# A three-phase transformer block on one core: the experts' first rows are added to x by accumulating transfers from GpSimd

## The reference, cut to what matters

```python
def reference(x, ...):                          # x: 32 x 256 x 128, float32 (8192 tokens)
    x = x + 0.5 * ffn(layernorm(x), ...)        # phase f1: 8 experts, 2 of them per token
    x = x + attn(layernorm(x), ...)             # phase at
    x = x + 0.5 * ffn(layernorm(x), ...)        # phase f2: as f1
    return x

def ffn(x, rw1, rb1, rw2, rb2, we1, be1, we2, be2):
    logits = silu(x @ rw1 + rb1) @ rw2 + rb2    # the two best of 8 experts per token
    w = softmax over the two best
    return x + sum over e of w[e] * (silu(x @ we1[e] + be1[e]) @ we2[e] + be2[e])

def attn(x, g1, b1, Wq, Wk, Wv, Wo, g2, b2, Wf1, Wf2):   # 32 sequences of 256 tokens
    x = x + linear_attention(layernorm(x, g1, b1))       # 16 heads of 64, causal
    return x + gelu(layernorm(x, g2, b2) @ Wf1) @ Wf2
```

## Time and profile before

| | |
|---|---|
| time, median of 3 runs | 2164.51 us (2164.07 to 2168.26) |
| the profiled execution, its own time | 2165.33 us |
| its span (first to last instruction) | 2163.3 us |
| granted TensorE clock, mean of the span | 0.923 |
| busy: TensorE, VectorE, ScalarE, GpSimd | 1727.8, 1517.6, 1041.2, 914.0 us |
| phase f1, at, f2 (from the timeline) | until about 509, to about 1610, to 2163 us |

### The profile page before, as it was taken

One profiled execution on the slowest core, in us unless ns is written; L12 is line 12 of the kernel. 1 busy time (PEld: TensorE's weight loads), 2 busy tenths in 40 slices (PEclk: granted clock), 3 DMA queues, 4 the chain that ended last, 5 costly groups with the idle time before them and its releaser, 6 DMA issues. The chain is left out here.

```text
span 2163.3 us, 36059 instructions
## 1 busy us (share of the span) xinstructions
PE 1727.8 (80%) x12483; PEld 1397.8 (65%) x12483; DVE 1517.6 (70%) x4134; ACT 1041.2 (48%) x1833; POOL 914.0 (42%) x1020
## 2 busy tenths in 40 slices
PE   3442999993999999999999999999954444999970
PEld 2331777772788888888888888888843333777750
DVE  6663777774787888788788887887636653777753
ACT  1210766663556555565555555565521112666650
POOL 5775355555322222222222222222106773555560
PEclk9999999996999999999999999999965556999995
DMA  5535576651000000000000000000001115666637
GB/s 163 184 127 178 183 251 232 231 184 51 6 11 11 6 11 11 6 11 11 7 11 11 6 11 11 2 1 2 2 0 40 48 49 187 229 217 232 224 122 235
DMA packets 89309, 190.28 MB, mean 88 GB/s; under 512 B 15869, under 2 KB 54442, under 8 KB 78122
## 3 DMA queue, kind: packets, MB, share of 16 engines
q1 hardware_dynamic: 60202, 141.68, 19.6%
q0 software_dynamic: 18176, 37.79, 5.1%
q10 hardware_dynamic: 10752, 8.52, 1.2%
HBM read 131.08 MB, written 56.85 MB: 87 GB/s over the span
## 5 line engine op out<-in xcount | busy, mean ns | idle before, releaser
L503 POOL DMA_INDIRECT expert_rows<-f_rows_out,f_dest x312 | 311.4, 998 | 291.3 <-DVE f_rows_out L722 218.4
L1178 POOL TENSOR_TENSOR at_sc<-at_sc 128x512 f32<-128x512 f32 x128 | 168.6, 1317 | 496.1 <-DVE at_sc L1283 496.1
L435 ACT ACTIVATE f_hid<-f_up_ps,f_w 128x512 f32<-128x512 f32 x312 | 214.7, 688 | 170.6 <-PE f_up_ps L344 160.5
L1275 DVE SCALAR_TENSOR_TENSOR at_qk<-at_exps,at_relus 128x512 f32<-128x512 f32 x256 | 192.4, 752 | 145.5 <-ACT at_relus L1114 145.2
L497 POOL DMA_INDIRECT sent_rows<-f_xn,f_slot x256 | 250.4, 978 | 92.3 <-issue 74.7
L1283 DVE TENSOR_TENSOR at_sc<-at_s_ps,at_mask 128x384 f32<-128x384 f32 x512 | 251.6, 549 | 1.2 <-PE at_s_ps L985 1.2
L699 DVE TENSOR_TENSOR f_hid_lo<-f_hid,f_hid_hi 128x512 fp32r<-128x512 f32 x312 | 208.2, 689 | 14.3
L982 PE MATMUL at_s_ps<-at_qk 64*128 64x256 f32 x1024 | 171.2, 411 | 7.0 <-issue 5.6
L1158 ACT ACTIVATE raw<-at_num_ps 128x512 f32<-128x512 f32 x128 | 76.3, 596 | 206.0 <-PE at_num_ps L1002 206.0
L1113 ACT ACTIVATE at_exps<-at_proj_ps 128x512 f32<-128x512 f32 x253 | 152.1, 601 | 34.7 <-PE at_proj_ps L965 27.6
L997 PE MATMUL at_num_ps<-at_sc,at_vals 128*64 128x256 f32 x1024 | 161.1, 393 | 0.3 <-DVE at_den L1360 0.3
(11 more groups left out here) (238 smaller groups left out, 4633.7 us busy)
## 6 DMA issues: line engine op xcount, KB each, us to landing
f_w<-split_weights SPq DMA_DIRECT2D x78, 1028.0 KB, 5.0
f_got<-sent_rows SPq DMA_DIRECT2D x78, 264.0 KB, 4.7
split_weights<-f_split SPq DMA_DIRECT2D x8, 1024.0 KB, 4.5
at_taken<-expert_rows SPq DMA_DIRECT2D x64, 128.0 KB, 2.1
f_w<-expert_rows SPq DMA_DIRECT2D x32, 256.0 KB, 4.0
expert_rows<-f_rows_out,f_dest POOLq DMA_INDIRECT x312, 3.3
sent_rows<-f_pads ACTq DMA_DIRECT2D x16, 264.0 KB
x<-in_L_attn_x SPq DMA_DIRECT2D x16, 256.0 KB, 4.1
```

Of the source, the lines that this page charges most:

```text
L435: A(hid[:, c, :], up_ps[n % 4][:, :], ACT.Silu, bias=w[:, i % RING_W, 4 * HID + c:4 * HID + c + 1].bitcast(FP32)).then_inc(s_silu, 1)
L503: g.indirect_dma_start(out=k.back[:, :], out_offset=bass.IndirectOffsetOnAxis(dest[:, i % RING_DEST, q:q + 1], 0), in_=rows_out[:, i % RIN ...
L1178: g.tensor_tensor(sc[:, n % RING_SC, :, 3, :], sc[:, n % RING_SC, :, 1, :], sc[:, n % RING_SC, :, 2, :], ALU.add).then_inc(s_sum, 1)
L1275: stt(full, exps[:, p % 2, :], 1.0, relus[:, p % 2, :], ALU.min, ALU.add).then_inc(s_phi, 1)
```

## The change

The loads by SP, the ring `taken` and GpSimd's additions go. In their place GpSimd issues, for each block, two transfers from `expert_rows` straight onto the block of `k.x` in SBUF, with `accum_op=ALU.add`: the transfer itself reads x, adds and writes. The second of a block waits on GpSimd until the first has landed (both touch the same bytes). One semaphore of four, `s_added[i % 4]`, counts 16 for each transfer, so 32 per block. In the loop the first part of block s + 3 is issued at unit 1 of step s and the second at unit 3. VectorE waits for 32 more on the block's semaphore where it waited for `s_added` before.

```diff
--- before.py
+++ after.py
@@ -764,7 +764,6 @@
     return sems
 
 
-RING_TAKEN = 4
 RING_SC = 6
 
 
@@ -823,15 +822,13 @@
         h2_hi, h2_lo = sb("h2_hi", [P, BT], FP32R), sb("h2_lo", [P, BT], FP32R)
         gel = sb("gel", [P, HC, BT])
         warm = sb("warm", [P, 2])
-        taken = sb("taken", [P, RING_TAKEN, 2, BT])
 
         s_ps = [ps(f"s{i}") for i in range(4)]
         proj_ps, num_ps, slot_ps = [ps(f"proj{i}") for i in range(2)], ps("num"), ps("slot")
 
         s_split_hi, s_split_lo, s_const, s_head_sel = (
             sem("split_hi"), sem("split_lo"), sem("const"), sem("head_sel"))
-        s_taken = [sem(f"taken{i}") for i in range(RING_TAKEN)]
-        s_first, s_added = sem("first"), sem("added")
+        s_added = [sem(f"added{i}") for i in range(4)]
         s_st = {n: sem(f"st{n}") for n in "ABC"}
         s_mv = {n: sem(f"mv{n}") for n in "ABC"}
         s_ve = {n: sem(f"ve{n}") for n in "ABC"}
@@ -891,16 +888,6 @@
             return ap.rearrange("p a b -> p (a b)")
 
         block = ctx.enter_context(nc.Block())
-
-        @block.sync
-        def _(sp):
-            for i in range(NB):
-                if i >= RING_TAKEN:
-                    sp.wait_ge(s_added, i - RING_TAKEN + 1)
-                for j in range(2):
-                    first = j * TOKENS + i * BT
-                    sp.dma_start(taken[:, i % RING_TAKEN, j, :],
-                                 k.back[first:first + BT, :].rearrange("(p q) d -> p (q d)", q=BQ)).then_inc(s_taken[i % RING_TAKEN], 16)
 
         @block.tensor
         def _(pe):
@@ -1177,15 +1164,17 @@
                 pool.wait_ge(s_masked, 2 * n + 2)
                 g.tensor_tensor(sc[:, n % RING_SC, :, 3, :], sc[:, n % RING_SC, :, 1, :], sc[:, n % RING_SC, :, 2, :], ALU.add).then_inc(s_sum, 1)
 
-            def add_back(i):
-
-                pool.wait_ge(s_taken[i % RING_TAKEN], 32 * (i // RING_TAKEN + 1))
-                g.tensor_tensor(k.x[:, xc(i)], k.x[:, xc(i)], taken[:, i % RING_TAKEN, 0, :], ALU.add).then_inc(s_first, 1)
-                pool.wait_ge(s_first, i + 1)
-                g.tensor_tensor(k.x[:, xc(i)], k.x[:, xc(i)], taken[:, i % RING_TAKEN, 1, :], ALU.add).then_inc(s_added, 1)
-
-            add_back(0)
-            add_back(1)
+            def add_back(i, j):
+
+                if j:
+                    pool.wait_ge(s_added[i % 4], 32 * (i // 4) + 16)
+                first = j * TOKENS + i * BT
+                g.dma_start(k.x[:, xc(i)], k.back[first:first + BT, :].rearrange("(p q) d -> p (q d)", q=BQ),
+                            accum_op=ALU.add).then_inc(s_added[i % 4], 16)
+
+            for j in range(2):
+                for i in range(2):
+                    add_back(i, j)
             inverse_std("A", 1)
             inverse_std("B", 1)
             inverse_std("A", 2)
@@ -1216,8 +1205,9 @@
                                     pattern=[[-1, UNITS], [-32, 2], [0, DH]], channel_multiplier=1).then_inc(s_const, 1)
             g.affine_select(out=low_rows_4[:, :], in_=low_rows_4[:, :], compare_op=ALU.is_ge, fill=0.0, base=31,
                             pattern=[[32, 4]], channel_multiplier=-1).then_inc(s_const, 1)
-            add_back(2)
+            add_back(2, 0)
             sum_blocks(0)
+            add_back(2, 1)
 
             for s in range(NB + 2):
                 for u in range(UNITS):
@@ -1230,8 +1220,8 @@
                         inverse_std("B", s + 3)
                     if u == 2 and has_rest(s):
                         inverse_std("C", s)
-                    if u == 3 and s + 3 < NB:
-                        add_back(s + 3)
+                    if u in (1, 3) and s + 3 < NB:
+                        add_back(s + 3, u // 2)
                 if s == 0:
                     nc.clear_and_free_semaphores(spent)
                     pool.sem_inc(k.cleared, 1)
@@ -1309,13 +1299,13 @@
                 return lambda q: k.x[:, xc(i, q)]
 
 
-            dve.wait_ge(s_added, 1)
+            dve.wait_ge(s_added[0], 32)
             first_mean("A", 0, x_of(0))
             low(0)
             normalise("A", 1, y_of(0), x_of(0), s_y)
             dve.wait_ge(s_y, 1)
             first_mean("B", 0, y_of(0))
-            dve.wait_ge(s_added, 2)
+            dve.wait_ge(s_added[1], 32)
             first_mean("A", 1, x_of(1))
             normalise("B", 1, lambda q: z[:, q, :], y_of(0), s_z)
             low(1)
@@ -1353,7 +1343,7 @@
                     if g + 1 < LAST:
                         mask_scores(2 * (g + 1))
                     if u == 0 and ahead:
-                        dve.wait_ge(s_added, s + 3)
+                        dve.wait_ge(s_added[(s + 2) % 4], 32 * ((s + 2) // 4 + 1))
                         stats("A", lambda q: k.x[:, xc(s + 2, q)])
                     if u == 0 and rest:
                         dve.wait_ge(s_quad, s)
```

## The result

The changed kernel takes 2169.8 us (median of 20 runs), the kernel before 2166.4 us in the same comparison (20 runs): ratio 1.0015, 95% interval 1.0009 to 1.0022, so 3.4 us longer, with 1.9 to 4.8 us in the interval. It is a small loss, 0.15% of the time, and clear of zero.

A forecast was written before the change was run, and what follows sets the result against it. The prediction took TensorE's own instructions to bound the attention phase, one pass in 32.8 us. Only the start counted, so 2164.5 + 0.6 = 2165.1 us; own range 2163.5 to 2171, 8 in 10 from 2162 to 2183.

The forecast's parts named there:

- The sum: Whole kernel: removed additions 0, issues 0, 29 passes 0, start +0.6 us, added to the median of 2164.5 us.
- Passes: 29 steady passes of the step loop: x may land up to 4.5 us after issue at no cost; value 0.
- the removed additions: GpSimd in the step loop: 32 pairs of 1.66 us, 53 us, end before idle time; value 0.
- the issues: GpSimd in the step loop: two DMA issues per pass, about 2 us, hidden in idle time; value 0.
- the landing: Steady passes: second transfer lands 3.2 us after issue, with 4.0 us of room before stats A; value 0.
- Rival (b): Steady passes: removing GpSimd's additions frees VectorE time that reaches TensorE, gaining 0.5 us a pass, 14.5 us; chance 0.06.
- Rival (c): GpSimd's transfer issue is held up by VectorE, landing at 3.6 us, +1.4 us, 2166; part of the forecast's 0.74.
- L: Time from start of a transfer's issue to landing in SBUF, sum made: 3.2 us taken, upper bound 4.6.
- The estimate of 2.6 us: Accumulating transfer by the Trainium skill: 2.0 + 0.6 us, which would turn the start into a 0.6 us gain.
- The start: Start of attention phase: two transfers in series before block 0's stats A; normalise at 517.9 against 517.26, +0.6 us.
- Rival (a): Stats A in every steady pass: landing above 4.5 us makes the kernel slower, +18.7 us at 5.0; chance 0.20.
- The slack: Steady passes: another 0.5 us behind the 4.0 us of room, before TensorE's broadcast at 1028.03 is late.

The follow-up runs named there:

- price: Changed kernel plus extra GpSimd transfers into unused columns; landing 2.6, 3.1 and 4.1 us for 64, 128 and 256 KB accumulated; no ratio given.
- half_start: Changed kernel, but second rows of blocks 0 and 1 loaded by SP and added by GpSimd; ratio 0.9987, stats A at 4.74 us.
- low_after: Changed kernel with VectorE's low(0) moved behind normalise of block 0; no ratio, first reciprocal at 59.96 us, last write of x at 1103.46 us.
- delay3: Changed kernel with three 0.9 us GpSimd memsets ahead of each pass's second transfer; last write of x +44.5 us against after_again.
- base_again: Unchanged copy of the kernel before, run again on later chips; ratio 1.0014 (0.9995 to 1.0033).
- after_again: Unchanged copy of the changed kernel, run again on later chips; ratio 1.0010 (0.9989 to 1.0031).
- order: Kernel before, with GpSimd's additions of block 1 moved behind inverse_std A of block 0 and low(0) behind its normalise; ratio 1.0005 (0.9989 to 1.0021).

## Why the prediction was right, and which of its terms were off

**The number.** The sum gave +0.6 us and the measurement +3.4. It stayed inside the forecast of 0.2% (4.3 us) because the range was wide enough for terms at the start that the sum had too small, not because the sum was close. A further 1.9 us of the distance between 2165.1 and 2169.8 is the reference: the kernel before has a median of 2164.5 in the three runs at hand and 2166.4 in the twenty of the comparison.

**Passes: right.** Value 0 for the removed additions (0.5 us of VectorE given back to its wait for ScalarE), 0 for the issues (0.9 us each, nobody behind them late), 0 for the landing (3.1 us taken in 4.0 us of room). Rival (b), a gain through VectorE, is refuted by the pass of 32.8 us. Rival (c), an issue held up by VectorE, doesn't show: the longest issue, 1.25 us, is the second of the phase, while VectorE is idle, and block 2's second issue, which starts at 542.13 beside VectorE's cast (L1330, 540.97 to 542.73), takes 0.90 us and lands after 3.1.

**L: right within 0.1 us.** 3.2 taken, 3.1 measured. The rows for twice the bytes gave a good value for this size; that twice the bytes is the reason, price doesn't show. The estimate of 2.6 us from the Trainium skill (DMA: Bandwidth & Descriptors, "Anatomy of one DMA", with Collectives: The Full Stack, "The bandwidth ceiling: the fold count and why AG ≠ RS ≠ AR") was 0.5 us short: its 2.3 us for a plain transfer of 128 KB agree with the 2.4 of L1237, but its two fetched sources don't cover the rest.

**The start: right in mechanism, short in size.** +0.6 was the sum, +2.1 us the measured shift of normalise. In the sum's own terms, from ScalarE's first instruction: GpSimd's first issue stands at 0.47 us, where -0.04 was taken (+0.5); the first transfer lands after the 3.2 us that were taken, but the issue that waits for it comes 0.26 us behind it instead of 0.1 (+0.2); from there to stats A 3.14 instead of 3.23 (-0.1); and from stats A to normalise 2.77 instead of 1.88 us (+0.9). The last is the mis-sized term. rs_A was laid under low(0), at its undisturbed duration; beside low(0), which reads two operands from SBUF, ve_A took 1.08 us and not 0.19. A row at hand had shown the same: the addition L1185 takes 1.69 us beside low(0) and 0.73 in a pass. The Trainium skill has this (SBUF — State Buffer, "Who interferes with whom": a VectorE instruction with two SBUF inputs contends with a GpSimd instruction that reads SBUF), and the runs agree: 1.08 beside it, also in half_start, where an addition and not an issue stands ahead of ve_A, and 0.19 without it in low_after. The prediction used the section for GpSimd's issues and not for its small operations. low_after also shows that taking these 0.9 us out doesn't shorten the phase, since low(0) itself then stands in the chain. And the prologue doesn't move as one, as the prediction had it: the shift of 2.1 us at normalise is 1.8 at the first reciprocal in the first pair, and 2.0 becomes 2.4 in the second (the last section).

**Rival (a): the right knee, the wrong victim.** It would have decided from a landing at about 4 us plus a slack. The slack was read at the broadcast (0.5 us). The one that is late first is `values`, behind den, and with the next use of raw behind it a pass absorbs some 0.2 us in delay3. VectorE's next wait for ScalarE shrinks only from 1.13 to 0.90 us there (a phi at 1043.62), since ScalarE's work is late as well.

**What stays open.** The phase is 2.0 us longer in the first pair of traces and 2.7 in the second, and copies of one kernel differ by up to 1.8. The rest of the 3.4 us lies inside the interval, 1.9 to 4.8; whether the unchanged phases give any of it can't be told.

## What to carry to other kernels

A dependency that costs nothing inside a loop (the second accumulation is issued over 12 us after the first) puts two full latencies in series where the pipeline starts; work out the prologue apart from the loop. An accumulating transfer of 128 KB from GpSimd (3.1 us) competes with a load and an addition (2.1 + 0.7 us), and this kernel has to keep two on the same bytes apart, while its two loads overlap. Engine time that is freed before a wait is only moved into that wait: look at the bracket of the next instruction before giving it a price. And a small operation laid under a neighbour (ve_A under low(0)) may take as long as the neighbour: look for a row of the pair before taking its undisturbed duration.

## What the runs showed of the hardware that was not expected

The distance at the start changes on its way to the loop. In base_again and after_again VectorE's cast L1340 (L1330 in the changed kernel) is 2.0 us apart (27.29 and 29.28 us after ScalarE's first instruction), the first reciprocal 2.4; in order the 0.57 us at the cast become 1.31. Between the two marks TensorE starts again after 5.6 us of idleness, at the 1.2 GHz level (a granted clock of 0.50), and the 2.4 GHz level comes back at different moments. Windows view of base_again, then order, 4.0 to 6.0 us after TensorE's first instruction there (the last three columns are clock, DMA share, GB/s):

```profile
559.33:561.33 2.00, 2.00 (x17) 1.54 (x14) 0.02 (x1) 0.60 (x1) 1.27 (x1) 0.91 0.00 0
```

```profile
566.79:568.79 2.00, 2.00 (x13) 1.29 (x12) 0.03 (x1) 0.26 (x1) 1.26 (x1) 0.50 0.00 0
```

In those 2 us the first runs mostly at 2.4 GHz and the second at half of it. In after_again the same window has 0.63. The time from TensorE's restart to the first reciprocal goes with it: 28.3 us in base_again, 28.7 in after_again, 29.0 in order. But the moment also differs between copies of one kernel: in the first pair the window has 1.00 in both, with 28.0 us in before and 27.7 in after. So a shift of the prologue can reach the loop some tenths smaller (2.1 to 1.8 us) or larger (0.6 to 1.3 us) than it was, and whether the shift itself or the execution sets the clock's return isn't shown.
